# Gates in three events instead of one per chunk, and the next chunk's sums and transposition two or three items further ahead

## The reference

```python
x = layernorm(x + attention0(x))
x = layernorm(x + experts(x))                  # token goes to 1 of 8 experts
# layer 1, attention: what is made here
q = rmsnorm(x @ Wq per head, q_rms_w)          # [B, T, 16, 64]
k = rmsnorm(x @ Wk per head, k_rms_w)
v = x @ Wv
gate = softplus(einsum(k, u / |u|) / sqrt(64)) # one value per token and head
omega_eff = softplus(omega) * slopes
bias = -(i - j) * omega_eff * gate[j]          # added to the scores, j <= i
```

## Time and profile before

| what | value |
|---|---|
| median of 3 runs | 2428.01 us (2422.49 to 2430.48) |
| profiled execution: time | 2427.31 us |
| profiled execution: span of the core | 2425.5 us |
| TensorE busy | 2123.1 us (88%) |
| VectorE, ScalarE, GpSimd busy | 1521.8, 1240.9, 776.8 us |
| granted TensorE clock, mean | 0.931 |
| last part of the middle stage | 777.2 to 1112.0 us of the span |

### The profile page before, as it was taken

One profiled execution on the slowest core, in us unless ns is written; L12 is line 12 of the kernel. 1 busy time (PEld: TensorE's weight loads), 2 busy tenths in 40 slices (PEclk: granted clock), 3 DMA queues, 4 the chain that ended last, 5 costly groups with the idle time before them and its releaser, 6 DMA issues.

```text
span 2425.5 us, 33799 instructions
## 1 busy us (share of the span) xinstructions
PE 2123.1 (88%) x11360; PEld 1179.7 (49%) x11408; DVE 1521.8 (63%) x3455; ACT 1240.9 (51%) x1955; POOL 776.8 (32%) x474
## 2 busy tenths in 40 slices
PE   5899999997397887882999999999999995899998
PEld 2333333334385444441555555555555553455554
DVE  3777777773432666664878878888888853333321
ACT  2366666665243777674455655665565551222322
POOL 5000000001501101000577777777777772000000
PEclk8899999998598888886799999999999997899999
DMA  4233332112174555558656665666566556354300
GB/s 166 84 122 122 122 121 107 55 41 95 54 198 112 176 167 166 163 163 206 162 147 160 167 168 141 171 172 153 149 173 171 143 170 166 78 127 107 79 9 9
DMA packets 230011, 319.08 MB, mean 132 GB/s; under 512 B 22200, under 2 KB 152504, under 8 KB 229444
## 3 DMA queue, kind: packets, MB, share of 16 engines
q1 hardware_dynamic: 214728, 289.17, 44.1%
q0 software_dynamic: 7472, 24.27, 2.8%
q10 hardware_dynamic: 7640, 3.48, 0.5%
HBM read 176.92 MB, written 105.84 MB: 117 GB/s over the span
## 4 chain that ended last, share of the span: by engine, by line
PE 26%; DVE 16%; issue 8%; DMA 2%; SPq 1%; ACT 0%; DVEq 0%
PE ps L1219 9%; DVE a1mx L926 4%; PE ps L872 3%; DVE a1KB L944 3%; DVE a1mx L930 3%; PE ps L856 3%; DVE a1QB L944 3%; PE ps L1170 2%; PE ps L857 2%; PE ps L828 2%; DVE a1mx L923 2%; DMA frec<-s_rec 1%; PE ps L1230 1%; PE ps L1208 1%; PE ps L1207 1%
## 5 line engine op out<-in xcount | busy, mean ns | idle before, releaser
L1054 POOL TENSOR_TENSOR a1sum<-a1sum,a1prob 128x1024 f32<-128x1024 f32 (+3 forms) x256 | 489.8, 1913 | 53.0 <-ACT a1prob L994 19.7
L994 ACT ACTIVATE a1prob<-ps 128x512 f32<-128x512 f32 (+2 forms) x640 | 325.4, 561 | 244.5 <-PE ps L859 235.0
L461 DVE TENSOR_REDUCE a0grid<-ps 128x8 f32<-128x1024 f32 x288 | 349.3, 1222 | 136.8 <-PE ps L337 74.5
L563 ACT ACTIVATE a0prob<-ps 128x1024 f32<-128x1024 f32 x288 | 292.0, 1024 | 192.2 <-PE ps L363 96.9
L923 DVE CUSTOM_DVE_ANT_0 ps<-ps,c_mask_ij 128x384 f32<-128x384 f32 (+5 forms) x512 | 271.3, 551 | 105.7 <-issue 104.2
L828 PE MATMUL ps<-a1KA,a1QA 68*128 68x384 f32 (+5 forms) x768 | 252.5, 397 | 56.7 <-DMA a1QA<-a1QB 27.2
L856 PE MATMUL ps<-a1QA,a1KA 69*128 69x512 f32 (+3 forms) x768 | 283.4, 377 | 1.7 <-DMA a1QA<-a1neg 1.7
L872 PE MATMUL ps<-a1prob,a1V 128*64 128x512 f32 (+3 forms) x1536 | 270.3, 494 | 0.0
L857 PE MATMUL ps<-a1QB,a1KB 128*128 128x512 f32 (+3 forms) x768 | 262.4, 349 | 0.0
L828 PEld LDWEIGHTS ps<-a1KA,a1QA 68*128 68x128 f32 x768 | 140.3, 199 | 110.3 <-DVE a1mx L926 50.7
L872 PEld LDWEIGHTS ps<-a1prob,a1V 128*64 128x64 f32 x1536 | 102.1, 137 | 165.4 <-issue 137.8
(11 more groups left out here) (254 smaller groups left out, 3385.0 us busy)
## 6 DMA issues: line engine op xcount, KB each, us to landing
a1FK<-s_k SPq DMA_DIRECT2D x128, 256.0 KB
a1FQ<-s_q SPq DMA_DIRECT2D x128, 256.0 KB
s_xs<-c_zero POOLq DMA_DIRECT2D x19, 1024.0 KB, 8.9
s_q<-mqkT SPq DMA_DIRECT2D x32, 512.0 KB
s_k<-mqkT SPq DMA_DIRECT2D x32, 512.0 KB
s_v<-mv SPq DMA_DIRECT2D x32, 512.0 KB, 4.1
a1V<-s_v SPq DMA_DIRECT2D x32, 512.0 KB, 4.6
a1KA<-a1KB SPq DMA_DIRECT2D x64, 256.0 KB
```

Source lines behind the costliest of these rows:

```text
L461: dve.tensor_reduce(grid[g % 2][:, :, a:b + 1:b - a], banks(("max", k)), axis=AX.X, op=ALU.max).then_inc(s1_free, 1)
L563: act.activation(prob[:, :, a:b + 1:b - a, :], banks(("exp", q)), ACT.Exp).then_inc(p_full, 1)
L994: act.activation(weights_of(g, u)[:, group[0]:group[-1] + 1, off:BANK], both(e, u, group), ACT.Exp).then_inc(weighed, 1)
L1054: pool.tensor_tensor(t[:, :, off:BANK], t[:, :, off:BANK], weights_of(g, u)[:, :, off:BANK], ALU.add).then_inc(summed, 1)
```

## The change

The gates of all chunks are no longer made one chunk at a time. `EVENTS = {24: range(0, 2), 72: range(2, 6), 96: range(6, 8)}`: in turn 24 those of chunks 0 and 1, in turn 72 of chunks 2 to 5, in turn 96 of chunks 6 and 7. `gates_a` and `soften` stand in that turn, `gates_b` three turns later (one turn later for the last event), on tiles of up to 128 x 256. The transpositions and copies of aug follow one chunk a turn, from four turns after the event (28, 29; 76 to 79), and for the last event both in turn 98; `send_gates` is issued in SyncE's queue two turns after the copy (in the last event, right at the end). z has room for all chunks, augT and its semaphore g_out have two buffers, aug and its helpers are four times as large.

`join` moves from turn 5 to 2, `root2` from 6 to 3, `norm` from 7 to 5, `xT` and `keep_x` from 8 to 6, `gate` and `keep_z` from 8 to 9. A Sqrt on one constant (`warm`) stands at the head of ScalarE's last part.

```diff
+        EVENTS = {24: range(0, 2), 72: range(2, 6), 96: range(6, 8)}
+        wide = TILES * max(len(cs) for cs in EVENTS.values())
+        zabs, g, gj = own("zabs", [P, wide, heads]), own("g", [P, wide, heads]), own("gj", [P, wide, heads])
+        z = own("z", [P, steps, TILES, heads])
+        aug, augT = own("aug", [P, wide, P // heads, heads], F32R), [own(f"augT{r}", [4 * heads, CHUNK]) for r in range(2)]
+        warm = own("warm", [P, 1])
...
+        turn_gates = {n: () for n in range(NI + TLAG)}
+        for n, cs in EVENTS.items():
+            if cs[-1] + 1 < steps:
+                turn_gates.update({n + 4 + k: (c,) for k, c in enumerate(cs)})
+            else:
+                turn_gates[n + 2] = tuple(cs)
...
-            elif n % 12 == 8 and n // 12 + 1 < steps:
-                here += [("xT", n // 12 + 1, 0), ("gate", n // 12 + 1, 0)]
-            if n % 12 == 4 and 0 <= n // 12 - 1 < steps:
-                here.append(("aug", n // 12 - 1, 0))
+            elif n % 12 in (6, 9) and n // 12 + 1 < steps:
+                here.append((("xT", "gate")[n % 12 // 9], n // 12 + 1, 0))
+            here += [("aug", c, 0) for c in turn_gates.get(n, ())]
...
-                if n % 12 == 5 and n // 12 > 0:
-                    send_gates(n // 12 - 1)
-            send_gates(steps - 1)
+                for c in turn_gates.get(n - 2, ()):
+                    send_gates(c)
+            for n in (NI + TLAG - 2, NI + TLAG - 1):
+                for c in turn_gates[n]:
+                    send_gates(c)
...
-            nc.sync.dma_start(scr["g1"][:, chunk(c)], augT[:, :]).then_inc(g_out, 16)
+            nc.sync.dma_start(scr["g1"][:, chunk(c)], augT[c % 2][:, :]).then_inc(g_out[c % 2], 16)
...
                 c, o = divmod(n, 12)
+                if o == 2 and c + 1 < steps:
+                    join(c + 1)
                 if o == 5 and c + 1 < steps:
-                    join(c + 1)
-                if o == 7 and c + 1 < steps:
                     norm(c + 1)
-                if o == 2 and c > 0:
-                    gates_a(c - 1)
-                if o == 3 and c > 0:
-                    gates_b(c - 1)
+                if n in EVENTS:
+                    gates_a(event_of[EVENTS[n][0]])
+                for late in (1, 3):
+                    if n - late in EVENTS and late == (3 if n - late + 4 < NI else 1):
+                        gates_b(event_of[EVENTS[n - late][0]])
...
             def keep_aug(c):
 
                 act.wait_ge(t_full, at["aug", c, 0] + 1)
-                if c > 0:
-                    act.wait_ge(g_out, 16 * c)
-                act.activation(augT[:, :], ps[0:4 * heads, 6 + at["aug", c, 0] % 2, :], ACT.Copy).then_inc(aug_kept, 1)
+                if c > 1:
+                    act.wait_ge(g_out[c % 2], 16 * (c // 2))
+                act.activation(augT[c % 2][:, :], ps[0:4 * heads, 6 + at["aug", c, 0] % 2, :], ACT.Copy).then_inc(aug_kept, 1)
 
             act.wait_ge(made, PREPARED)
+            act.activation(warm[:, :], eps[:, :], ACT.Sqrt)
...
+                if o == 3 and c + 1 < steps:
+                    root2(c + 1)
                 if o == 6 and c + 1 < steps:
-                    root2(c + 1)
-                if o == 8 and c + 1 < steps:
                     keep_x(c + 1)
+                if o == 9 and c + 1 < steps:
                     keep_z(c + 1)
-                if o == 2 and c > 0:
-                    soften(c - 1)
-                if o == 4 and c > 0:
-                    keep_aug(c - 1)
+                if n in EVENTS:
+                    soften(event_of[EVENTS[n][0]])
+                for c in turn_gates.get(n, ()):
+                    keep_aug(c)
```

More of the change, by code:

```diff
@@ L1871, in middle @@
         ss_full, z_scaled, gated, soft, aug_full = sem("ss_full"), sem("z_scaled"), sem("gated"), sem("soft"), sem("aug_full")
-        qk_out, v_out, g_out = [sem(f"qk_out{r}") for r in range(2)], [sem(f"v_out{r}") for r in range(2)], sem("g_out")
+        qk_out, v_out, g_out = ([sem(f"{n}{r}") for r in range(2)] for n in ("qk_out", "v_out", "g_out"))
         NI = 3 * NTILE
@@ L1877, in middle @@
         TLAG = 3
+        events = [EVENTS[n] for n in sorted(EVENTS)]
+        event_of = {c: k for k, cs in enumerate(events) for c in cs}
+        place_of = {c: (c - cs[0]) * TILES for cs in events for c in cs}
+        turn_gates = {n: () for n in range(NI + TLAG)}
[4 more added lines that the diff above has]
+                turn_gates[n + 2] = tuple(cs)
         line = []
@@ L1919, in sync_last @@
                 sp.wait_ge(qk_out[r], 32 * NTILE // 2)
-            sp.wait_ge(g_out, 16 * steps)
+                sp.wait_ge(g_out[r], 16 * steps // 2)
         def send_gates(c):
             nc.sync.wait_ge(aug_kept, c + 1)
-            nc.sync.dma_start(scr["g1"][:, chunk(c)], augT[:, :]).then_inc(g_out, 16)
+            nc.sync.dma_start(scr["g1"][:, chunk(c)], augT[c % 2][:, :]).then_inc(g_out[c % 2], 16)
         def gpsimd_last():
@@ L1964, in job @@
                 else:
-                    pe.wait_ge(aug_full, a + 1)
+                    pe.wait_ge(aug_full, event_of[a] + 1)
                     for t in range(TILES):
-                        end = pe.transpose(bank[:, t * P:(t + 1) * P], aug[:, t, :, :].rearrange("p a h -> p (a h)").bitcast(F32), ident)
+                        end = pe.transpose(bank[:, t * P:(t + 1) * P], aug[:, place_of[a] + t, :, :].rearrange("p a h -> p (a h)").bitcast(F32), ident)
                 end.then_inc(t_full, 1)
@@ L2004, in tensor_last @@
                     k += 1
-            job(k)
         def pair(n):
@@ L2073, in gates_b, with parts, gates_a @@
-            def gates_b(c):
-                n = [GSTEP * c + 1]
+            def parts(k):
+                cs = events[k]
+                n = len(cs) * TILES
+                return n, z[:, cs[0]:cs[-1] + 1, :, :].rearrange("p c t h -> p (c t) h"), zabs[:, 0:n, :], g[:, 0:n, :], gj[:, 0:n, :]
+            def gates_a(k):
+                n, zs, za, _, _ = parts(k)
+                dve.wait_ge(z_scaled, (events[k][-1] + 1) * TILES)
+                if k > 0:
+                    dve.wait_ge(gated, GSTEP * k)
+                dve.scalar_tensor_tensor(za, zs, -1.0, zs, ALU.mult, ALU.max).then_inc(gated, 1)
@@ L2077, in then, with gates_b @@
+            def gates_b(k):
+                count = [GSTEP * k + 1]
                 def then(instruction):
-                    n[0] += 1
+                    count[0] += 1
                     instruction.then_inc(gated, 1)
[L2080 to L2091, removed]
+                    dve.wait_ge(gated, count[0])
@@ new lines, in gates_b @@
+                n, zs, za, gs, gjs = parts(k)
+                cs = events[k]
+                dve.wait_ge(soft, 2 * k + 2)
+                then(dve.scalar_tensor_tensor(gs, zs, 0.0, za, ALU.max, ALU.add))
+                then(dve.tensor_tensor(gs, gs, om[:, :].unsqueeze(1).to_broadcast([P, n, heads]), ALU.mult))
+                then(dve.tensor_tensor(gjs, gs, jpos[:, cs[0]:cs[-1] + 1, :].rearrange("p c t -> p (c t)").unsqueeze(2).to_broadcast([P, n, heads]), ALU.mult))
+                if k > 0:
+                    dve.wait_ge(t_full, at["aug", cs[0] - 1, 0] + 1)
@@ L2092, in gates_b @@
+                then(dve.tensor_copy(aug[:, 0:n, 0, :], gs))
+                then(dve.tensor_copy(aug[:, 0:n, 2, :], gjs))
+                then(dve.tensor_tensor(aug[:, 0:n, 1, :], gs, aug[:, 0:n, 0, :].bitcast(F32), ALU.subtract))
+                then(dve.tensor_tensor(aug[:, 0:n, 3, :], gjs, aug[:, 0:n, 2, :].bitcast(F32), ALU.subtract))
                 dve.sem_inc(aug_full, 1)
```

29 lines of the change are left out of this document (8 added, 21 removed).

## The result

| | before | changed |
|---|---|---|
| median of the runs | 2428.24 us (4 runs, 2422.49 to 2430.48) | 2388.52 us (4 runs, 2385.38 to 2391.97) |
| ratio, 95% interval | | 0.9832 (0.9814 to 0.9849) |
| profiled execution: time, span | 2427.31, 2425.5 us | 2385.38, 2383.6 us |
| mean granted clock | 0.931 | 0.942 |

39.7 us less, where 34 were forecast; the time lies in the range, and in the forecast's own range. The windows of the changed kernel come first: the last part from its first q product to the next stage, a chunk without gates, the three slow stretches inside it, and the chunks of the first and of the second event (columns as in the earlier trace rows).

A forecast was written before the change was run, and what follows sets the result against it. TensorE was taken to bound the kernel, VectorE and ScalarE closely behind, with losses once per chunk. Terms -1.3 - 29.6 + 0.2 - 2.4 = -33.1 us took 2427.3 to 2394, range 2374 to 2413.

The forecast's parts named there:

- the events: Gates of the last part made in three batches instead of seven: 53.4 us goes, 23.8 comes, -29.6.
- the tail: End of the last part: loads sooner, but longer operations and more transpositions, copies and transfers: +0.2 us.
- the transposition and the gate product: Next chunk's two jobs, moved behind q items: 5.7 us a chunk against 5.74 before; -2.4 us, mostly the first chunk's.
- the warm Sqrt: Before the last part's first norm: the first Sqrt's table load runs while ScalarE is idle, -1.3 us.
- Loads: ScalarE's table loads in the last part: 9 instead of 23 + 1, each 1.283 us, without a drain.
- The first event: Gates of chunks 0 and 1 at item 24: 6.65 us lost plus 1.7 for the clock, 8.3 us.
- The second event: Gates of chunks 2 to 5 at item 72: 13.3 us plus 2.2 for the clock, 15.5 us.
- the walk: Stepping through engine queues: for the next chunk's transposition, bank free at 18.4, norm ends 18.95, start 19.1 us.
- The first rival: Steps ahead do hide the next chunk's transposition and gate product: -19 to -31 us more, about 2371; chance 0.18.
- 5.7 against 5.74: Cost per chunk of the next chunk's transposition and gate product, in us: new order against the kernel before.
- The third rival: Each chunk's two bank waits behind q items drop the clock: +43 us, slower at 2437; chance 0.03.
- The fourth: Table loads don't move the end; three batches of gates cost as much as seven: 2425 us; chance 0.05.

The follow-up runs named there:

- the places behind v items: Changed kernel with the next chunk's transposition behind item 8 and its gate product behind item 11, both v items: 2371.59 us, 0.9758.
- without tables: Kernel before with Copy in place of Exp and Ln in the gates, softplus left out: 2401.6 us, 0.9886.

## Why the prediction was right, point by point

The range and the direction are right, the parts less so. Of the -41.9 us of the last part the events brought -30.3 by the rows (7.62 go seven times, 8.2 and 14.8 come; forecast -29.6) and the tail -0.3 (+0.2); what is left, -11.3, is the transposition and the gate product (-2.4). Outside it the warm Sqrt brought -1.2 (-1.3), and what comes behind took 1.2 more.

- **Loads: right.** 9 instead of 24, no drain behind them (idle 0.1 us for three): the 2.66 us that the Trainium skill counts for a switch ("ScalarE: Activation LUTs", "What ACT_TABLE_LOAD costs") is not what a run here shows, the 1.283 us of the load itself is.
- **The first event: right, the clock in part by luck.** 10.5 us from item 24 to item 27 were forecast, the rows show 854.24 - 843.69 = 10.55; the event costs 40.43 - 32.21 = 8.2 us, forecast 8.3. The second wait was 2.35 instead of 2.9. I had a long slow stretch half hidden by it, 1.7 us; it was one of 3.42 us with none of it hidden, which is 1.7 too. In the kernel with four buffers the same stretch was hidden, and the event cost 6.5, near the 6.65 without the clock.
- **The second event: the total right, its two halves wrong by about as much.** 14.8 us, forecast 15.5. Six waits were forecast (3.6, 3.8, 1.4, 1.35, 0.4 and 2.4 us, 12.95 in all); the rows have 3.71, 1.96, 0.91, 2.01, 1.02 and 0.82, 10.4 in all. For the clock I had 2.2 us; TensorE was busy 3.41 and 5.81 us at half clock, which costs about half of that, 4.6 us (an estimate). The new wait on the landing is there and on the path, as the four buffers show; with 3.41 and 4.38 us it is longer than the 2.8 and 3.5 I had, because the copies go on only 3.8 and 3.9 us after SyncE's issues at 1007.77 and 1014.84, where I took 3.5, and are ready for them sooner.
- **Transposition and gate product: the size wrong, and this is where the missing us lie.** I had 5.7 us a chunk, it is 4.6. The waits are 1.1 less (0.17 instead of 0.6 behind the join, 1.56 instead of 2.1, 0.82 instead of 0.95), the 0.7 for the clock went unspent, and the jobs with their hand-overs take 0.7 more than the 1.33 I had. 7 x 1.1 = 7.7 us. The order that the walk gave, bank first and norm last, is the one in the rows. The first rival's 2371 was not reached here; the places behind v items are what reached it.
- **The baseline of that term.** "5.7 against 5.74" (measured 4.6 against 5.74) holds the new order against the kernel before, where the gates' stall hid the join, and so says that the steps ahead bring nothing. The runs showed that they are worth 17.3 us once the gates are gone, and the gates' removal 24.6 without them. The prediction names nothing of this. The sum came near because it stepped through the new order as a whole and compared whole chunks, and did not add up edits.
- **Warm Sqrt: right by the trace.** The load runs at 761.43; the first q product comes 1.2 us sooner (777.70, 778.92).
- **Tail:** +0.2 forecast. From the last v product to the next stage 15.16 us instead of 15.46: -0.3.
- **The third rival** (the clock falls at short waits behind q items) did not come: window 898.25 to 930.46 has 1.00, with waits of 1.56 and 0.82 us 8 us apart (forecast 2.1 and 0.95). What the Trainium skill warns of in "TensorE: Matmul & The Clock Gate" ("A second HAM failure mode: psum-queue depth-cycling"), a clock that goes up and down with short idles from cycling the banks, these chunks don't show. It did fall behind 1.21 and 0.78 us close together, but those waits are for the normalized tile and the kept transposition, not for banks.
- **The fourth** (the loads don't move the end) is refuted: without tables the last part of the kernel before is 28.0 us shorter.

Open: why the slow stretch of the first event begins ahead of the second wait in one kernel and behind it in another with the same order around it; and what of the 13.5 us comes from norm being sooner and what from the two jobs standing apart.

## What to carry to other kernels

Stalls hide work: a step that costs nothing beside one stall can delay others once that stall is gone (here 1.1 us a chunk), so rate a set of edits by stepping through the new order as a whole, and time halves only to learn which of them carry each other. Put extra jobs of a shared bank ring where the neighbours leave both banks free. Keep two unavoidable waits apart: close together they cost the clock as well in all seven chunks of the kernel before, and 8 us apart in none of the changed kernel's chunks without gates. When a row names one engine for a wait with several conditions, look at the end of each. When work is batched, look for the buffer whose turnaround is now a transfer's landing: here two buffers for four chunks cost 5 us, two more buffers gave it back.

## What the runs showed of the hardware that I had not expected

- The clock carried more than the waits: of 41.9 us in the last part 26.2 are the same matmul records taking less time.
- The same waits may or may not cost the clock. In the kernel with the join added to the events, 1.21 and 0.78 us of waiting were followed by a q product at half clock (3.39 us, above), while in another of its chunks 1.53 and 0.78 us were not (1.96 us):

```profile
880.19 0.63 PE L1971 MATMUL ps<-c_ident,mxout 128*128 128x128 f32 x4 [1.53 <-DVE mxout L2051]
...
882.48 1.96 PE L2008 MATMUL ps<-mwq,mflip 128*128 128x512 f32 x4
```
